# First router of a macaron block: centred gate as the stationary operand, and output stores of four tiles

## The reference

```
x = x + 0.5 * ffn(layernorm(x))     # "f1" in the kernel
x = x + attention(layernorm(x))     # 8 heads of 64, low-rank keys and values
x = x + 0.5 * ffn(layernorm(x))     # "f2", same weights as f1

layernorm(x) = (x - mean) / sqrt(var + 1e-5)
ffn(h): logits = h @ gate_w.T       # (tokens, 8)
        sel, top = argmax, max of the 8 logits
        xs = h * sigmoid(top)       # for the tokens of expert e
        out = (xs @ w_up[e].T * silu(xs @ w_gate[e].T)) @ w_down[e].T
```

## Time and profile before

| | us |
|---|---|
| median of 3 runs (1203.85 to 1205.66) | 1205.15 |
| the profiled execution's own time | 1205.7 |
| its span, first to last instruction | 1203.9 |
| PE busy in the span | 984.3 |
| DVE busy | 735.9 |
| POOL busy | 676.9 |
| ACT busy | 483.2 |

### The profile page before, as it was taken

The page is one execution under the profiler, slowest core; times in us unless marked ns, Lnnn a source line. Parts: engine busy times, 40 slices in busy tenths (PEclk is TensorE's granted clock), DMA queues, the critical chain, the costliest instruction groups (busy, mean ns, idle before and its releaser), DMA issues.

```text
span 1203.9 us, 17005 instructions
## 1 busy us (share of the span) xinstructions
PE 984.3 (82%) x5096; PEld 551.8 (46%) x5097; DVE 735.9 (61%) x1195; ACT 483.2 (40%) x760; POOL 676.9 (56%) x385
## 2 busy tenths in 40 slices
PE   5839975399999989999988999998999999469700
PEld 4828842144444454434454444445344555448600
DVE  6565556747677745667774677777566735555431
ACT  1253431154444434444434444442355653444300
POOL 0025452267868717768754777773587885045371
PEclk9999967599999989999999999999899999569955
DMA  8054532100000100000010000001002000145453
GB/s 292 0 171 149 146 95 91 39 1 1 1 2 1 62 1 1 1 1 1 1 62 2 1 1 1 1 1 62 1 1 106 2 1 1 63 144 162 131 151 120
DMA packets 40046, 62.22 MB, mean 52 GB/s; under 512 B 5936, under 2 KB 33072, under 8 KB 38960
## 3 DMA queue, kind: packets, MB, share of 16 engines
q1 hardware_dynamic: 20000, 27.40, 6.4%
q0 software_dynamic: 6912, 18.88, 5.8%
q10 hardware_dynamic: 13072, 15.09, 3.6%
HBM read 30.81 MB, written 23.07 MB: 45 GB/s over the span
## 4 chain that ended last, share of the span: by engine, by line
PE 63%; DVE 16%; issue 8%; ACT 5%; DMA 3%; POOL 1%; DVEq 1%; ACTq 0%; POOLq 0%; SPq 0%
PE ps_o L949 16%; PE ps L936 9%; PE ps L731 7%; PE ps L571 6%; DVE maxes L737 5%; DVE rows_store L1259 5%; PE ps_x L711 4%; PE ps L1082 3%; PE ps L208 2%; PE ps_x L970 2%; ACT rows_store L487 2%; PE ps L555 2%; PE ps_o L587 1%; PE ps_x L587 1%; PE ps L223 1%
## 5 line engine op out<-in xcount | busy, mean ns | idle before, releaser
L737 DVE TENSOR_REDUCE maxes<-ps 128x2 f32<-128x1024 f32 x256 | 311.9, 1218 | 213.9 <-PE ps L731 211.4
L1342 POOL TENSOR_TENSOR arena_b<-arena_b 128x1024 f32<-128x1024 f32 x112 | 268.3, 2396 | 164.1 <-PE ps_o L949 123.1
L1342 POOL TENSOR_TENSOR arena_b<-arena_b,hot_store 128x1024 f32<-128x1024 f32 x112 | 268.8, 2400 | 84.1 <-ACT hot_store L1140 42.1
L936 PE MATMUL ps<-q_split,keys_now 64*128 64x512 f32 x1536 | 207.2, 395 | 0.0
L1140 ACT ACTIVATE arena_b<-ps 128x1024 f32<-128x1024 f32 x144 | 144.4, 1023 | 104.3 <-PE ps L936 104.1
L520 POOL DMA_INDIRECT arena_b<-scaled_x,token_of x80 | 75.7, 947 | 179.3 <-issue 81.7
L936 PEld LDWEIGHTS ps<-q_split,keys_now 64*128 64x128 f32 x1536 | 147.5, 188 | 31.7 <-issue 2.4
L949 PE MATMUL ps_o<-arena_b,latent_now 128*64 128x512 f32 x576 | 148.9, 617 | 3.1 <-ACT arena_b L1140 0.4
L1140 ACT ACTIVATE hot_store<-ps 128x1024 f32<-128x1024 f32 x112 | 111.9, 1022 | 54.9 <-PE ps L936 54.7
L1259 DVE RECIPROCAL rows_store<-rows_store 128x256 f32<-128x256 f32 (+1 forms) x72 | 112.6, 1565 | 12.0 <-ACT rows_store L1151 12.0
L949 PE MATMUL ps_o<-hot_store,latent_now 128*64 128x512 f32 x448 | 116.6, 617 | 3.3 <-ACT hot_store L1140 0.9
(11 more groups left out here) (182 smaller groups left out, 1145.8 us busy)
## 6 DMA issues: line engine op xcount, KB each, us to landing
sorted_y<-arena_b ACTq DMA_DIRECT2D x80, 128.0 KB
scaled_x<-rows_store SPq DMA_DIRECT2D x32, 256.0 KB, 2.1
x_res<-x_in SPq DMA_DIRECT2D x4, 1024.0 KB, 13.0
keys_now<-keys_next SPq DMA_DIRECT2D x4, 1024.0 KB, 4.6
out<-x_res SPq DMA_DIRECT2D x32, 128.0 KB
arena_a<-w_gu SPq DMA_DIRECT2D x1, 2048.0 KB, 15.9
keys_max_now<-keys_max_next SPq DMA_DIRECT2D x4, 512.0 KB, 5.4
arena_a<-w_gu ACTq DMA_DIRECT2D x1, 2048.0 KB, 7.7
```

Of the source, the lines that this page charges most:

```text
L737: nc.vector.tensor_reduce(maxes[:, 2 * m:2 * m + 2], ps[2][:, :, :], AX_X, ALU.max) \
L936: last = nc.tensor.matmul(ps_s[n % 2][:, a, :], keys_now[h, key, k], query[h, p, q], start=False, stop=(kt >= KT - STRIDE and query is q_h ...
L1342: nc.gpsimd.tensor_tensor(t, t, prob(k, kt).rearrange("p a n -> p (a n)"), ALU.add) \
```

## The change

Two places are changed.

The router of f1 no longer normalises rows before it turns them. Let w be the gate. Since the logit of a token is (x - mean) . w / std, and (x - mean) . w = x . (w - mean of w), the kernel subtracts from each expert's column of the gate its mean over the 256 numbers (`gate_c`, made once by two small matmuls with a matrix of ones and one DVE instruction) and multiplies raw rows by it; the argmax needs no 1/std, and the top logit alone is multiplied by it. PE turns raw tiles of `x_res`, four at a time (a group of 512 tokens, two banks of PSUM, `turn`), ACT copies each bank to `x_cols`, and the gate, padded with zeros to 32 columns (`QUAD`), is now the stationary operand: a matmul moves 512 tokens and writes 8 rows of logits in a quarter of 32 partitions of a bank. Two groups are multiplied in turn, each in its own quarter (`logits_of`). Four groups fill a bank; ACT copies it to SBUF (`copy_rows`), PE turns it back with four transposes (`back`), and DVE copies the logits out. The statistics of all 32 tiles are finished in one go, with one square root. The router of f2 is as before.

The output stores of f2 are now written out instead of looped over: seven DMAs of four tiles (512 KB), then four of one tile.

```diff
+GROUP = 4
+GROUPS = NT // GROUP
+QUAD = 32
+STORE = 4
...
+        gate_c = sb("gate_c", [P, DC, QUAD])
...
+        x_cols = [arena_b[:, 2560 + n * DC * HALF:2560 + (n + 1) * DC * HALF].rearrange("p (c n) -> p c n", c=DC)
+                  for n in range(4)]
+        logit_rows = arena_b[:, 6656:6656 + 2 * HALF].rearrange("p (g n) -> p g n", g=2)
...
+        def pe_router(pe):
+
+            for c in range(DC):
+                last = nc.tensor.matmul(banks[4][:, 0:EXPERTS], ones[:, :], gate_w[:, c, :],
+                                        start=(c == 0), stop=(c == DC - 1))
+            last.then_inc(sem("gate_sum"), 1)
+
+            def turn(q):
+                if q >= 2:
+                    pe.wait_ge(sem("x_copied"), DC * (q - 1))
+                for c in range(DC):
+                    for j in range(GROUP):
+                        x = x_tile(GROUP * q + j)[:, c * P:(c + 1) * P]
+                        last = nc.tensor.transpose(banks[2 * (q % 2) + c][:, j * P:(j + 1) * P], x, ident[:, :])
+                    last.then_inc(sem("x_turned"), 1)
+
+            def logits_of(q0):
+
+                pe.wait_ge(sem("x_copied"), DC * (q0 + 2))
+                for c in range(DC):
+                    for q in (q0, q0 + 1):
+                        rows = slice(QUAD * (q % 4), QUAD * (q % 4 + 1))
+                        last = nc.tensor.matmul(banks[6 + q // 4][rows, :], gate_c[:, c, :], x_cols[q % 4][:, c, :],
+                                                start=(c == 0), stop=(c == DC - 1))
+                last.then_inc(sem("logit_rows"), 1)
+
+            def back(n):
+                pe.wait_ge(sem("logit_rows_copied"), n + 1)
+                for i in range(GROUP):
+                    last = nc.tensor.transpose(banks[4 + n][:, i * P:(i + 1) * P],
+                                               logit_rows[:, n, i * P:(i + 1) * P], ident[:, :])
+                last.then_inc(sem("logit_f1"), 1)
+            for g in range(LOADS):
+                pe.wait_ge(sem(f"x_loaded{g}"), 16)
+                turn(2 * g)
+                turn(2 * g + 1)
+                if g:
+                    if g == 1:
+                        pe.wait_ge(sem("gate_ready"), 1)
+                    logits_of(2 * g - 2)
+                if g == LOADS - 1:
+                    back(0)
+            logits_of(GROUPS - 2)
+            back(1)
+
+        def act_router(act):
+            def copy_rows(n):
+                act.wait_ge(sem("logit_rows"), 2 * n + 2)
+                nc.scalar.activation(logit_rows[:, n, :], banks[6 + n], ACT.Copy).then_inc(sem("logit_rows_copied"), 1)
+            for q in range(GROUPS):
+                for c in range(DC):
+                    act.wait_ge(sem("x_turned"), DC * q + c + 1)
+                    if q >= 4:
+
+                        act.wait_ge(sem("logit_rows"), (q - 4) // 2 + 1)
+                    nc.scalar.activation(x_cols[q % 4][:, c, :], banks[2 * (q % 2) + c], ACT.Copy) \
+                        .then_inc(sem("x_copied"), 1)
+                if q == GROUPS - 1:
+                    copy_rows(0)
+            act_std(act, "f1")
+            copy_rows(1)
+
+        def dve_router(dve):
+            dve.wait_ge(sem("gate_sum"), 1)
+            dve.wait_ge(sem("consts_loaded"), 48)
+            dve.wait_ge(sem("gate_zeroed"), 1)
+            nc.vector.scalar_tensor_tensor(
+                gate_c[:, :, 0:EXPERTS], banks[4][:, 0:EXPERTS].unsqueeze(1).to_broadcast([P, DC, EXPERTS]), -1.0 / D,
+                gate_w[:, :, :], ALU.mult, ALU.add).then_inc(sem("gate_ready"), 1)
+            for g in range(LOADS):
+                dve.wait_ge(sem(f"x_loaded{g}"), 16)
+                with dve.Fori(g * NT // LOADS, (g + 1) * NT // LOADS) as t:
+                    tile_stats(t, "f1")
+            dve_stats(dve, "f1", 0, NT)
...
+                for n in range(2):
+
+                    dve.wait_ge(sem("logit_f1"), n + 1)
+                    half = logits[:, n * NT * EXPERTS // 2:(n + 1) * NT * EXPERTS // 2]
+                    ins = nc.vector.tensor_copy(
+                        half.rearrange("p (g i e) -> p g i e", g=4, i=GROUP),
+                        banks[4 + n].rearrange("p (i g w) -> p g i w", i=GROUP, w=QUAD)[:, :, :, 0:EXPERTS])
+                    if n:
+                        link(ins)
+            lg = logits[:, :].rearrange("p (t e) -> p t e", e=EXPERTS)
             link(nc.vector.tensor_reduce(top, lg, AX_X, ALU.max))
...
+                nc.vector.tensor_tensor(st[:, 7, :], top, st[:, 4, :], ALU.mult).then_inc(sem("top_f1"), 1)
...
-            with sp.Fori(0, NT) as t:
-                col = sp.snap(t * D)
-                sp.wait_ge(sem("ffn_added_f2"), t + 1)
-                sp.dma_start(out_tiles[:, ds(t, 1), :], x_res[:, ds(col, D)].unsqueeze(1)) \
+            stores = [(t, STORE) for t in range(0, NT - STORE, STORE)] + [(t, 1) for t in range(NT - STORE, NT)]
+            for t, n in stores:
+                sp.wait_ge(sem("ffn_added_f2"), t + n)
+                sp.dma_start(out_tiles[:, t:t + n, :],
+                             x_res[:, t * D:(t + n) * D].rearrange("p (t d) -> p t d", d=D)) \
                     .then_inc(sem("out_stored"), 16)
-            sp.wait_ge(sem("out_stored"), 16 * NT)
+            sp.wait_ge(sem("out_stored"), 16 * len(stores))
...
+            pool.memset(gate_c[:, :, :], 0.0).then_inc(sem("gate_zeroed"), 1)
```

More of the change, by code:

```diff
@@ L211, in logit @@
                 last.then_inc(sem(f"logit_{tag}"), 1)
-            start = EARLY if tag == "f2" else 0
+            start = EARLY
             def body(i, first):
@@ L229, in body @@
                         logit(i - 1, 1)
-            if tag == "f1":
-                each(pe, NT // 4, body)
-            else:
-                for i in range(start // 2, NT // 4):
-                    body(i, False)
+            for i in range(start // 2, NT // 4):
+                body(i, False)
             logit(NT // 4 - 1, 1)
@@ L246, in body @@
                     nc.scalar.activation(x_col[:, k, :], banks[k], ACT.Copy).then_inc(sem(f"col_ready_{tag}"), 1)
[L247 to L257 removed]
+            for i in range(EARLY // 2, NT // 4):
+                body(i, False)
         def dve_rows(dve, tag):
@@ L268, in body @@
                             .then_inc(sem(f"row_ready_{tag}"), 1)
-            if tag == "f1":
-                def arrived(g):
-                    dve.wait_ge(sem(f"x_loaded{g}"), 16)
-                    with dve.Fori(g * NT // LOADS, (g + 1) * NT // LOADS) as t:
-                        tile_stats(t, tag)
-                arrived(0)
-                for g in range(LOADS):
-                    t0, t1 = g * NT // LOADS, (g + 1) * NT // LOADS
-                    dve_stats(dve, tag, t0, t1, g)
-                    for i in range(t0 // 4, t1 // 4):
-                        body(i, i == 0)
-                        if i == t0 // 4 and g + 1 < LOADS:
-                            arrived(g + 1)
-            else:
-                dve_stats(dve, tag, 2 * EARLY, NT, 1)
-                for i in range(EARLY // 2, NT // 4):
-                    body(i, False)
+            dve_stats(dve, tag, 2 * EARLY, NT, 1)
+            for i in range(EARLY // 2, NT // 4):
+                body(i, False)
         link_count = [0]
@@ L339, in dve_route @@
             wide = [P, NT, EXPERTS]
-            dve.wait_ge(sem(f"logit_{tag}"), NT // 2)
-            lg = banks[2][:, 0:NT * EXPERTS]
             if tag == "f2":
+                dve.wait_ge(sem("logit_f2"), NT // 2)
                 late = slice(2 * EARLY * EXPERTS, NT * EXPERTS)
-                link(nc.vector.tensor_copy(logits[:, late], lg[:, late]))
-                lg = logits[:, :]
-            lg = lg.rearrange("p (t e) -> p t e", e=EXPERTS)
+                link(nc.vector.tensor_copy(logits[:, late], banks[2][:, late]))
+            else:
+                for n in range(2):
[7 more added lines that the diff above has]
+            lg = logits[:, :].rearrange("p (t e) -> p t e", e=EXPERTS)
             link(nc.vector.tensor_reduce(top, lg, AX_X, ALU.max))
-            nc.vector.tensor_copy(st[:, 7, :], top).then_inc(sem(f"top_{tag}"), 1)
+            if tag == "f2":
+                nc.vector.tensor_copy(st[:, 7, :], top).then_inc(sem("top_f2"), 1)
+            else:
+                nc.vector.tensor_tensor(st[:, 7, :], top, st[:, 4, :], ALU.mult).then_inc(sem("top_f1"), 1)
             link(nc.vector.tensor_tensor(rank, lg, top.unsqueeze(2).to_broadcast(wide), ALU.is_equal))
@@ L1421, in _ @@
             for tag in ("f1", "f2"):
-                dve_rows(dve, tag)
                 if tag == "f1":
+                    dve_router(dve)
                     dve.wait_ge(sem("masks"), 3)
                     dve.wait_ge(sem("tables"), 3)
+                else:
+                    dve_rows(dve, tag)
                 ends = dve_route(dve, tag)
```

15 lines of the change are left out of this document (2 added, 13 removed).

## The result

| | before | after |
|---|---|---|
| median of 4 runs each | 1205.41 us (1203.85 to 1206.19) | 1166.77 us (1165.18 to 1167.11) |
| ratio | | 0.9678, 95% interval 0.9662 to 0.9695 |
| the profiled execution, its span | 1205.7, 1203.9 | 1166.87, 1164.7 |

The forecast was 1163.6 with a gain of 41.5; the profiled executions differ by 39.2 in span. The likeliest case came, 3 us short. Outside the span the profiled execution has 2.2 us, where it had 1.8.

What follows compares the result with a forecast made beforehand. PE's instruction count at the low clock, after a late start, bounded f1's router; SP's store backlog bounded the end. Gains of 23.2 + 18.3 = 41.5 us gave 1163.6 us, own range 1160 to 1168, 8 in 10 from 1159.5 to 1176.

Steps and rivals of the forecast that it cites:

- PE's start: f1's router: PE waits for constants alone and starts when the kvd loads land, between 9.0 and 9.6, taken as 9.3 us.
- Transposes: f1's router on PE: 64 transposes, at 0.22 us each on the lower clock level and 0.11 on the upper.
- Logits: f1's router on PE: 32 matmul instructions of 512 columns, 0.25 us each on the upper clock level, 0.50 on the lower.
- Rival B: f1's router: logit matmuls in different quarters of the array don't overlap, 9 us more, time 1173; chance 6%.
- The rise of the clock: f1's router: PE's clock goes from lower to upper level at 18 to 19 us, so PE is done at 30.2.
- Rival A: f1's router: PE's clock stays low throughout, reduce at 43.3, gain only 11.7 us, time 1175.1; chance 22%.
- DVE's floor: f1's router: DVE's statistics, variance and the wait for ACT's root let the scale be done no earlier than 30.0 us.
- Carried to the end: After f1's router: the rest of the route waits only for the reduce, so the 23.2 us gain carries to the end.
- SP's backlog: f2's output stores: SP's slow state strikes instructions, not bytes; with 11 instructions SP keeps up, gaining 18.3 us.
- rival C: f2's output stores: the stores themselves are slow under the gathers; tail gains 0 to 11 us, time 1171 to 1182; chance 9%.
- The failed step: Program end: the span ends 2.1 us after the last store's issue, new end taken as 1185.6, 18.3 us gained.
- D: f1's experts: PE stays at the lower clock level after a shorter router, up to 70 us more, time 1234; chance 2%.

## Why the prediction was right, and where not

- *PE's start* was taken at 9.3 on kvd's load and came at 9.70.
- *Transposes* at 0.22 and 0.11 us: 0.22 and 0.12 measured.
- *Logits* at 0.25 an instruction on the upper level: 0.23. Rival B, no overlap, is out.
- *The rise of the clock* I put at 18 to 19 us; it came near 13.7, or 16.5 in others. This term was mis-sized: the 32 transposes were over at 15.9 and not at 17.2, the first eight logit instructions took 1.91 and not 3.0. I had weighed, where transposes ran at the low level, 4.43 us busy of 6.00, as if their kind might count. The changed kernel and the one with gaps show that for transposes it is the gaps. Rival A is out. By the rule of the Trainium skill (TensorE: Matmul & The Clock Gate, Part 4: PE-mode transpose) transposes don't count as activity, and the level should have stayed low until 15.83; 230 ns that turn into 140 near 13.7 us speak against it for gapless float32 transposes. The measurement decides.
- *DVE's floor* of 30.0 was real in size: the scale ended at 29.88, and with PE's last logits at 27.6, DVE became last. The way to it was partly luck, two errors that cancel: I had the variance at 27.2 and the root held up to 28.5 by ACT's copies and table load; in truth the table was loaded by 25.96, and the variance came at 28.11. Gain 24.5, forecast 23.2: 1.3 too little.
- *Carried to the end*: 23.6 at f1's first gather, 24.3 at f2's route, 24.4 at f2's first gather. Right, though the scatter found above (before and after both had the long wait) is wide enough that this closeness is partly luck.
- *SP's backlog*: right in that it strikes instructions, not bytes (rival C is out with 4.20 MB moved at 25%), and more narrowly than I had it, as stores with a constant address were never slow. Right in size as well: SP was through at 1161.1, and by my working for the tail, counted from a last add at 1159.23, it would be 1159.23 + 2.1 = 1161.3. The last add was 1.2 us later behind the last gather than before, the upper end of what I had allowed (1.1).
- *The failed step* is the end: "the span ends 2.1 later". I let SP's end be the program's end and didn't ask what else ended under its cover. POOL's DRAIN stood there, until 1189.1 in before, and the stores' new end lay ahead of it: 14.5 us gained instead of 18.3. With the DRAIN in it, my sum would have been 23.2 + 14.5 = 37.7 and the time near 1167.5, against 1166.77. The forecast missed by only 3 us because the two errors are of opposite sign: 3.8 too much at the end, 1.3 to 1.5 too little ahead of it.
- D, slower through the experts' clock, didn't come: PE did 15 instructions in the 5.0 us up to 65.0 and 27 in the 4.8 us from 65.2 on; in the kernel before it was 15 in the 5.6 us up to 89.6 and 29 in the 5.2 us from 89.8 on, the same turn 24.6 us later.

## What to carry to other kernels

When a backlog that ends the program is removed, list what every engine still does under it, closing instructions too: the next end is the latest of those. While POOL issues gathers, give the stores of other engines constant addresses; a few rounds of a loop may fit, too. When two profiles of the same code differ by microseconds, look for one short instruction with two lengths. Start work on raw data as soon as it lands and keep it free of gaps; then check what lands next before moving a start forward once more.

## What the runs showed of the hardware

- Under f2's gathers each instruction with registers on SP or ACT, branches and counters too, came to take 0.69 to 0.73 us, most 1.4 us after the start of the one ahead. Before and after, most such instructions took 29 to 75 ns, and an issue of one tile with its address in registers 338 to 368 ns. Stores with constant addresses took 332 ns (one tile) to 382 (four) throughout. The slow state began 12 to 17 us after the first gather and outlasted the last gather's issue by 3.2 to 4.7 us. What resource they contend for was not found.
- POOL's closing DRAIN ended 8.8 us after POOL's last instruction in all 14 profiles, behind a gather in thirteen and behind a memset in one.
- Float32 transposes without a gap raised the clock 2.8 to 6.0 us after they began; with a gap of 0.69 us after every four they did not in 13 us, yet such gaps didn't lower it afterwards. In the kernel begun early the level rose 3.0 us into its first run of transposes (weight loads of 188 ns at 9.89 us), was still up after the pause of 2.4 us that followed (140 ns at 12.7 us), and fell at 13.4, 0.7 us after PE had begun again, until 16.8.
- A DVE SCALAR_TENSOR_TENSOR of 128x24 took 2.25 to 2.31 us when it began 0.07 to 0.13 us after a TENSOR_TENSOR of POOL (nine profiles), ending 0.04 us behind it, and 0.18 us when it began 0.02 to 0.04 us before it (five profiles).
- The stretch from f1's first gather to f2's route, unchanged, took 879.8 to 887.5 us in the 12 profiles with the new router.
